# GpSimd's mask multiply in a two-layer masked attention kernel: one operation over 1024 columns, or two over 512

## The reference

```python
qkv = layer_norm(x, g1, be1) @ w_qkv              # 8 heads of 16
scores = jnp.einsum('nhd,mhd->hnm', q, k) * SCALE
scores = jnp.where(adj != 0, scores, -jnp.inf)
attn = jax.nn.softmax(scores, axis=-1)
out = jnp.einsum('hnm,mhd->nhd', attn, v).reshape(n, DIM)
x = x + out @ w_proj + b_proj
x = x + jax.nn.gelu(layer_norm(x, g2, be2) @ w1 + b1) @ w2 + b2
```

## Time and profile before

| | us |
|---|---|
| three runs | 3652.48, 3656.32, 3665.82 |
| median | 3656.32 |
| the profiled execution, whole time | 3654.05 |
| its span, first to last instruction | 3652.3 |
| attention, first layer, from the first exponential's end | about 206 to 1726 |
| attention, second layer | about 2038 to 3537 |

### The profile page before, as it was taken

How to read it: one execution, slowest core, us unless ns; L and a number is a source line. 1 busy time by engine, 2 the same in 40 slices (tenths; PEclk the granted TensorE clock), 3 DMA queues, 4 the chain that set the end, 5 groups by cost and what they waited for, 6 DMA issues and landing times.

```text
span 3652.3 us, 68569 instructions
## 1 busy us (share of the span) xinstructions
PE 3436.8 (94%) x22572; PEld 1388.6 (38%) x22572; DVE 2968.7 (81%) x8997; ACT 2337.5 (64%) x2596; POOL 2489.9 (68%) x1476
## 2 busy tenths in 40 slices
PE   6999999999999999998869999999999999999988
PEld 3443333333333333332634433333333333333326
DVE  6889888888988898870568998999999989999604
ACT  4348686877777777866341466666666666666753
POOL 1057878787878787878110587787888787878870
PEclk9589999999999999999896799999999999999989
DMA  3578787878786869683232546454555555555432
GB/s 131 179 225 261 239 267 226 274 227 281 218 285 210 290 211 295 200 254 94 78 113 84 176 140 187 141 175 154 171 163 169 162 164 165 161 171 157 145 96 67
DMA packets 480351, 676.31 MB, mean 185 GB/s; under 512 B 51552, under 2 KB 272864, under 8 KB 475616
## 3 DMA queue, kind: packets, MB, share of 16 engines
q1 hardware_dynamic: 479568, 671.83, 59.2%
q10 hardware_dynamic: 432, 0.10, 0.0%
HBM read 508.14 MB, written 165.68 MB: 184 GB/s over the span
## 4 chain that ended last, share of the span: by engine, by line
PE 41%; POOL 36%; issue 13%; DVE 7%; DMA 2%; POOLq 1%; ACT 1%; DVEq 0%; SPq 0%; ACTq 0%
POOL arena L929 36%; PE PS L463 13%; PE PS L443 10%; PE PS L476 7%; PE PS L470 7%; DVE spill L806 5%; PE PS L416 3%; POOLq L907 1%; PE PS L449 1%; DVE arena L766 0%; PE PS L586 0%; DMA arena<-out_dram 0%; PE PS L407 0%; ACT o_sb L679 0%; DMA mask<-in_adj_t 0%
## 5 line engine op out<-in xcount | busy, mean ns | idle before, releaser
L806 DVE CUSTOM_DVE_ANT_0 spill<-PS,mask_n 128x512 bf16<-128x512 f32 x4096 | 2635.8, 688 | 278.0 <-PE PS L443 177.4
L671 ACT ACTIVATE arena<-PS 128x1024 f32<-128x1024 f32 x2048 | 1991.8, 1022 | 911.3 <-PE PS L476 870.4
L929 POOL TENSOR_TENSOR arena<-arena,mask 128x1024 int32<-128x1024 int32 x896 | 2136.8, 2385 | 638.0 <-ACT arena L671 633.0
L443 PE MATMUL PS<-k_t,q_t 48*128 48x512 f32 x4096 | 1288.3, 547 | 60.1 <-DVE pmax L806 40.2
L463 PE MATMUL PS<-arena,v_sb 128*32 128x512 f32 x8192 | 1099.4, 609 | 41.6 <-ACT o_sb L679 37.5
L470 PE MATMUL PS<-q_t,k_t 50*128 50x512 f32 x4096 | 934.3, 466 | 0.3 <-POOL arena L919 0.2
L443 PEld LDWEIGHTS PS<-k_t,q_t 48*128 48x128 f32 x4096 | 545.6, 194 | 1022.9 <-DVE pmax L806 911.8
L476 PE MATMUL PS<-arena,idb 64*128 64x512 bf16 x4312 | 841.8, 391 | 0.0
L470 PEld LDWEIGHTS PS<-q_t,k_t 50*128 50x128 f32 x4096 | 400.1, 188 | 199.6 <-ACT arena L671 121.7
L476 PEld LDWEIGHTS PS<-arena,idb 64*128 64x128 bf16 x4312 | 208.9, 95 | 465.5 <-issue 343.3
L806 DVE DVE_READ_ACCUMULATOR2_ANT pmax<- 128x1 f32 x4096 | 340.0, 83 | 0.0
(11 more groups left out here) (54 smaller groups left out, 979.9 us busy)
## 6 DMA issues: line engine op xcount, KB each, us to landing
mask<-m_dram SPq DMA_DIRECT2D x768, 256.0 KB, 2.7
mask_n<-mn_dram SPq DMA_DIRECT2D x768, 128.0 KB, 2.7
adj_in<-in_adj SPq DMA_DIRECT2D x256, 256.0 KB, 3.9
mask<-in_adj_t SPq DMA_DIRECT2D x256, 256.0 KB, 4.0
m_dram<-mask SPq DMA_DIRECT2D x256, 256.0 KB, 3.6
mn_dram<-mask_n SPq DMA_DIRECT2D x256, 128.0 KB, 3.8
mt_dram<-arena SPq DMA_DIRECT2D x256, 128.0 KB, 3.5
arena<-mt_dram SPq DMA_DIRECT2D x256, 128.0 KB, 2.8
```

Source lines behind the costliest of these rows:

```text
L443: pe.matmul(bank, q_t[r0:r0 + KROWS, gb % Q_SLOTS, pair, q * P:(q + 1) * P], k_t[r0:r0 + KROWS, pair, mb * TILE:(mb + 1) * TILE], start=Tr ...
L671: nc.scalar.activation(p_buf[:, t % P_SLOTS, 2 * half:2 * half + 2, :], ps_b[:, 2 * half:2 * half + 2, :], ACT.Exp, scale=SCALE).then_inc( ...
L806: dve.tensor_tensor_reduce(spill[:, j % A_BANKS, :], ps_a[:, j % A_BANKS, :], mask_n[:, v % N_SLOTS, :], 1.0, LOWEST, ALU.subtract, ALU.ma ...
L929: pool.tensor_tensor(p, p, m, ALU.mult).then_inc(p_masked, 1)
```

## The change

mask_pair issues two operations, one for head 2 and one for head 3, each over 512 columns of p_buf and the 512 columns of the mask, with no broadcast. The first carries POOL's waits, the second increments p_masked. Nothing else is changed: the number of increments, the waits of PE and SP and the data are the same.

```diff
                 else:
                     pool.wait_ge(adjt_loaded[t % M_SLOTS], fills(L, t) * 16)
-                p = p_buf[:, t % P_SLOTS, 2:4, :].bitcast(I32)
-                m = mask01[:, t % M_SLOTS, :].rearrange("p (a c) -> p a c", a=1).broadcast_to([P, 2, TILE])
-                pool.tensor_tensor(p, p, m, ALU.mult).then_inc(p_masked, 1)
+                for j in (2, 3):
+                    p = p_buf[:, t % P_SLOTS, j, :].bitcast(I32)
+                    last = pool.tensor_tensor(p, p, mask01[:, t % M_SLOTS, :], ALU.mult)
+                last.then_inc(p_masked, 1)
```

## The result

The changed kernel takes 3679.45 us (median of 5 runs, 3673.60 to 3682.82) against 3656.38 for the kernel before (5 runs). The ratio is 1.0059, with a 95% interval of 1.0041 to 1.0077: slower by 0.6%, 23 us. It lies within the range of 3655 to 3682 and near its upper end. The forecast of 3668 had half of the growth: +11.5 us where +23 was measured, and the outcome is just past the 0.5% beyond which I had put a chance of 0.20.

What follows compares the result with a forecast made beforehand. The prediction took DVE to pace ordinary steps and PE the tails, with POOL nearly level there. Tails +11.0 us and first-quad passes +0.5 made +11.5, giving 3668 us, range 3655 to 3682.

Steps and rivals of the forecast that it cites:

- the tails: Steps after the first sweep runs out of jobs: POOL becomes the bound, 5.5 us per tail, 11.0 us for two.
- The reading of the two regimes: Attention: DVE sets ordinary steps at 2.77 us, leaving POOL 0.38 of room; in tails PE sets 2.40, leaving 0.01.
- The term f: Fixed part of one more POOL instruction per step, taken as 0.23 us from the tensor_scalar over 4 columns.
- my own formula: Growth of the tails from POOL's spacing: 29f - 1.15 us per layer, 58f - 2.3 for both.
- First-quad passes: First layer, passes of the first quad: late masks cost between 0 and 3 us in all, taken as 0.5.
- DVE: ... there is nothing to gain or lose there: DVE beside POOL's multiply: its work doesn't stretch the multiply, 2380 ns with DVE idle and 2385 over all; cost nothing.
- PE's clock (rival 4): In the tail PE stands still 0.19 us in 2.59 and falls to 1.2 GHz, costing tens of us; chance 0.03.
- Rivals 1 to 3: Beside rival 1: 2, dearer tails only, 3675 to 3678, chance 0.08; 3, POOL bounds ordinary steps, about 3746, 0.10.
- rival 1: POOL's fixed part mostly overlapped or broadcast dearer, f of 0.15 or less: nothing happens, 3656 to 3663; chance 0.22.
- theory F: Account from the experiments, not the prediction: PE's wait at a change of pass brings the half clock; no chance given.

Runs made afterwards that it cites:

- tail_only: Kernel before with the multiply split only from step 476 on, in both layers; 3665.6 us, 1.0020 of before.
- ordinary_only: Kernel before with the multiply split only in steps before 476 outside the first layer's first-quad passes; 3666.7 us, 1.0023 of before.
- first_quad_only: Kernel before with the multiply split only in the first layer's first-quad passes, 128 of 896 multiplies; 3665.8 us, 1.0018 of before.
- four_pieces: Kernel before with the multiply in four operations of 256 columns; 3719.0 us, 1.0169 of before.
- before_longer_chain: Kernel before with one more tensor_reduce, its result unused, behind DVE's chain at the end of each first-sweep pass; 3681.0 us, 1.0064 of before.

## Why the prediction was right or wrong

The range held the time and the sign was right, but the sum was right for half of the growth, and that half was not made of the parts I had named at their sizes. That the range held it is in part luck: the tails grew by 6.5 us less than forecast, while some 15 us came from places where I had put 0.5 us or nothing.

- **The reading of the two regimes**: right. Ordinary steps stayed at 2.77 us, the tails became POOL's, and tail_only shows +2.26 us for each to the hundredth.
- **The term f**: mis-sized. I put 0.23 us less 0.03 of overlap, a spacing of 2.59; measured were 1.24 us from piece to piece and 2.47 for the pair. With 2.47 my own formula gives 28 x 0.07 + 0.15 = 2.1 us per tail, and 2.26 was measured; with 2.59 I had 5.5. The nearest row, the tensor_scalar over 4 columns, was a duration, and what counts is start to start. The memsets' rows already said that the two differ; I used them only for the lower end. The Trainium skill's 2.6 cycles a column at 1.2 GHz (GPSIMD Engine Reference, section "Performance versus the Vector engine"), from which I had estimated f = 166 ns, is borne out: 2.15 ns measured against its 2.17, and 0.14 us against 0.166. The estimate of 273 ns from its 4497 ns is not, though that figure itself lies within 1% of the 4.54 us that 0.14 us and 2.15 ns a column give for 2048 columns: the small difference of two long durations was a poor measure of f.
- **First-quad passes**: 0.5 us, measured +2.1 (0.6), within the 0 to 3 that I gave as bounds.
- **"DVE: ... there is nothing to gain or lose there"**: this is the step that failed. I checked whether DVE's work stretches POOL's and stopped there. The other direction costs: DVE's cast at a change of pass stands still until POOL's operation ends, the pair ends 0.15 us later, and PE waits for DVE. That is the +2.9 us of ordinary_only. The groups of the trace of before held the hint, a cast of 16 columns with a mean of 741 ns:

```profile
L814 DVE CAST neg_hi<-neg 128x16 fp32r<-128x16 f32 x32 | 23.7, 741 | 2.4
```

- **PE's clock (rival 4)**: wrong place. The tails of the changed kernel kept the full clock from step 483 on, in both of its traces. The clock fell at the changes of pass and between the stages, already before, and more often with the longer wait: 28 us more at half clock, 12 us of time. This is the largest single term, and nothing in my sum had it. That it is the wait that brings it is shown by the two kernels that change the wait alone.
- **Rivals 1 to 3**: by its price f lay in rival 1's corner (2.36 + f = 2.47 gives f = 0.11), for which I had +4 us; so rival 1 was right on POOL and wrong on the time, which the two missing terms brought. The sign that I named for it, two multiplies in under 2.36 us, was too narrow: rival 1 reached to f = 0.15, which is 2.51.
- **What would show it**: I named 1.31 us for an operation (1.287), tail steps 2.59 apart (2.47), and some 10 us of waits of PE for the multiply (5.7, most of it invisible to that view).

In part open remains why the time at half clock also rose in tail_only, by 9 us (standard error 5), and in first_quad_only, by 11 us (3.5), which for the latter is hardly chance. Their traces fit theory F: the commonest wait is 1.37 us in place of 1.35, and in the first layer some waits are long, in tail_only 1.28 and 1.34 us where before has 0.83 and 0.89. Whether the edit made these longer or they vary from one execution to the next, a single trace of each can't say. Between the layers and at the end of the program half-clock stretches also come and go from one execution to the next (114 to 119 us for the part after the last gather), and these have nothing to do with split_neg.

## What to carry to other kernels

Splitting a GpSimd operation in two costs one fixed part, 0.14 us here, on GpSimd itself, and where another engine sets the pace that part is hidden; look for the stretches where the engines are level, not at its mean share. Then ask who stands still while GpSimd runs: search the groups for DVE operations on few columns that take far longer than they should, and see whether they end when GpSimd's do. Where TensorE waits for a short serial chain on another engine, the chain costs more than its length when the clock falls behind it; here shortening it took TensorE's wait from 1.35 to 0.60 us at most changes of pass, 17 us in all, and brought 41 us.

## What the runs showed of the hardware

- A DVE cast or copy of 16 columns from SBUF to SBUF, 0.17 to 0.18 us with GpSimd idle, is not done while a GpSimd tensor_tensor is running and ends 0.03 to 0.04 us after it. A subtraction of two such inputs, 0.18 us otherwise, takes up to 0.78 us beside the pieces of four_pieces and 0.62 us beside an operation that makes masks (line 919). tensor_reduce on DVE is not held up (0.28 us beside a multiply and without).
- A GpSimd tensor_tensor of int32: 0.14 us and 2.15 ns for a column, start to start, from 256 and 512 columns, and 1024 lie on the same line; the record shows 1.287 us for 512 columns where the next starts after 1.24. Reading the second input by a broadcast costs nothing that shows (2.35 us against 2.34).
- In the trace of before PE stood still for 1.35 us (once 1.17) at each change of pass of the second layer from 2117 on. Behind 10 of these 14 waits the granted clock was at its lower level (1.2 GHz) for 3.4 us, which made such a pass 1.6 us longer. In the changed kernel, with mostly 1.52 or 1.49 us, it was 12 of 14 in each trace, in before_longer_chain, with 1.56 us or more, 14 of 14. With waits of mostly 0.60 us it was none of 28 in two traces; the one such stretch there within the second layer's passes began 22 us after its change of pass.
